# Fourth product of the linear cross-attention: two 128x128 products per batch against eight 32x32 products on the diagonal of the TensorE array

## The reference, cut to what matters

```python
Q, K, V = heads(ln(x) @ wq.T + bq), heads(c @ wk.T + bk), heads(c @ wv.T + bv)
score = einsum('bhqd,bhkd->bhqk', Q, K) / dk
ctx = einsum('bhqk,bhkd->bhqd', where(mask, -inf, score), V)
x = x + layernorm(ln(x) + ctx @ wo.T + bo)
```

## Time and profile before

| | |
|---|---|
| Median of 3 runs | 236.91 us (235.99 to 237.01) |
| Profiled execution, its own time | 236.04 us |
| Span in the profile | 234.2 us |
| TensorE busy | 220.6 us, 94% of the span |
| VectorE busy | 172.2 us, 74% |
| ScalarE busy | 125.0 us, 53% |
| GpSimd busy | 75.9 us, 32% |
| Granted TensorE clock | 0.998 of full speed (2.4 GHz) |

### The profile page before, as it was taken

One profiled execution on the slowest core, in us unless ns is written; L12 is line 12 of the kernel. 1 busy time (PEld: TensorE's weight loads), 2 busy tenths in 40 slices (PEclk: granted clock), 3 DMA queues, 4 the chain that ended last, 5 costly groups with the idle time before them and its releaser, 6 DMA issues.

```text
span 234.2 us, 5963 instructions
## 1 busy us (share of the span) xinstructions
PE 220.6 (94%) x2424; PEld 198.3 (85%) x2424; DVE 172.2 (74%) x370; ACT 125.0 (53%) x245; POOL 75.9 (32%) x101
## 2 busy tenths in 40 slices
PE   6998999999999998899999999999999999999991
PEld 6988798999999987778988999987778889988881
DVE  0669885886697699997975888978797674377353
ACT  3662961448346577757166798865643455740000
POOL 3012242030521617403526546693810022421011
PEclk9999999999999999999999999999999999999999
DMA  6799998986321613061302213032000000000001
GB/s 217 252 296 395 326 386 259 328 299 198 100 60 48 219 48 84 20 212 62 92 3 49 77 60 92 0 99 84 0 3 0 3 0 3 0 3 22 3 0 67
DMA packets 9435, 26.17 MB, mean 112 GB/s; under 512 B 1464, under 2 KB 2880, under 8 KB 9280
## 3 DMA queue, kind: packets, MB, share of 16 engines
q1 hardware_dynamic: 9120, 25.27, 32.9%
q10 hardware_dynamic: 288, 0.52, 0.6%
HBM read 25.27 MB, written 0.52 MB: 110 GB/s over the span
## 4 chain that ended last, share of the span: by engine, by line
PE 77%; DVE 6%; DMA 5%; ACT 5%; issue 4%; SPq 1%; POOLq 0%; POOL 0%; DVEq 0%; ACTq 0%
PE ps L707 72%; PE ps L710 5%; DMA w<-in_w 3%; DMA raw<-in_ctx 3%; ACT probT L518 1%; ACT ch L585 1%; DVE swapped L1258 1%; DVE straight L1262 1%; DVE straight L1259 1%; DVE mx L1232 1%; DVE prob L1242 1%; DVE swapped L1261 1%; ACT aT L518 1%; DVE sm L1240 0%; DVE Z L1304 0%
## 5 line engine op out<-in xcount | busy, mean ns | idle before, releaser
L707 PE MATMUL ps<-ch 128*128 128x130 f32 (+1 forms) x208 | 53.4, 272 | 1.6 <-DVE cl L1154 1.2
L707 PE MATMUL ps<-ch,cl 128*128 128x260 f32 (+1 forms) x208 | 52.1, 308 | 0.0
L707 PE MATMUL ps<-w,hT 128*128 128x512 f32 (+1 forms) x204 | 46.1, 382 | 0.0
L473 POOL TENSOR_TENSOR rstd<-ve,half_exp 128x1 f32<-128x1 f32 (+1 forms) x22 | 13.8, 626 | 88.6 <-DVE ve L1033 88.5
L707 PEld LDWEIGHTS ps<-w,hT 128*128 128x128 f32 x204 | 36.3, 188 | 7.2 <-issue 0.2
L707 PEld LDWEIGHTS ps<-ch 128*128 128x128 f32 (+1 forms) x208 | 39.6, 190 | 2.9 <-ACT ch L585 1.4
L1154 DVE TENSOR_TENSOR cl<-raw,ch 128x1024 fp32r<-128x1024 f32 (+4 forms) x31 | 31.8, 1056 | 10.9 <-ACT ch L585 10.6
L707 PEld LDWEIGHTS ps<-ch,cl 128*128 128x128 f32 (+1 forms) x208 | 39.2, 189 | 0.3
L585 ACT ACTIVATE ch<-raw 128x1024 fp32r<-128x1024 f32 (+4 forms) x31 | 27.4, 917 | 9.6 <-DMA raw<-in_ctx 8.4
L707 PE MATMUL ps<-xHL,dense 128*128 128x256 f32 x192 | 24.6, 285 | 0.0
L707 PEld LDWEIGHTS ps<-xHL,dense 128*128 128x128 f32 x192 | 23.5, 191 | 0.3
(11 more groups left out here) (157 smaller groups left out, 402.4 us busy)
## 6 DMA issues: line engine op xcount, KB each, us to landing
raw<-in_ctx SPq DMA_DIRECT2D x22, 512.0 KB, 4.4
raw<-in_w SPq DMA_DIRECT2D x8, 512.0 KB, 3.5
stage<-in_dense SPq DMA_DIRECT2D x4, 512.0 KB, 6.8
w<-in_w SPq DMA_DIRECT2D x4, 256.0 KB, 6.9
w<-in_w SPq DMA_DIRECT2D x1, 1024.0 KB, 8.6
mask<-in_mask SPq DMA_DIRECT2D x1, 800.5 KB, 7.6
raw<-in_ctx SPq DMA_DIRECT2D x8, 65.0 KB
raw<-in_ctx ACTq DMA_DIRECT2D x2, 256.0 KB, 4.8
```

The costliest lines, as they stand in the source:

```text
L473: pool.tensor_tensor(rstd[:, lo:hi], ve[:, lo:hi], half_exp[:, lo:hi], ALU.pow).then_inc(sem("rstd"), 1)
L707: return pe.matmul(o, l, r, start=start, stop=stop, skip_group_check=not check)
```

## The change

The matrix is kept as 32 columns per row, which is what `cross3` leaves: row `p` of `mb` holds the 32x32 block that its 32 rows share. A new constant `pair_heads` of 32 columns takes the place of `heads` at this spot (`heads` stays for another use, line 560). `cross4` then makes eight products per batch, one for each half and each group of 32 rows; product `r` reads rows `32r` to `32r+31` of `mb` and `q0T` and writes the same partitions of the bank. The list of steps, the semaphores and all other steps stay.

```diff
-for _name, _width in ((...), ("heads", P), ("causal", S), ...
+for _name, _width in ((...), ("heads", P), ("pair_heads", PAIR), ("causal", S), ...
...
+    put("pair_heads", ((p[:, None] // HD) % 2 == np.arange(PAIR)[None, :] // HD) * XSCALE)
...
-    mb, nxt = place("mb", [P, KC, P], at=nxt)
+    mb, nxt = place("mb", [P, KC, PAIR], at=nxt)
...
                     for ob in range(KC):
-                        last = mm(ps[:, CROSS_B[1], ob * S:(ob + 1) * S], mb[:, ob, :], q0T[:, ob, i * S:(i + 1) * S],
-                                  True, True)
+                        for r in range(P // PAIR):
+                            own_rows = slice(r * PAIR, (r + 1) * PAIR)
+                            last = mm(ps[own_rows, CROSS_B[1], ob * S:(ob + 1) * S], mb[own_rows, ob, :],
+                                      q0T[own_rows, ob, i * S:(i + 1) * S], True, True)
                     last.then_inc(sem("ctx"), 1)
...
                     pairs = ps[:, CROSS_B[0], D:D + KC * PAIR].rearrange("p (c n) -> p c n", c=KC)
-                    dve.tensor_tensor(mb[:, :, :].rearrange("p c (r n) -> p c r n", n=PAIR),
-                                      pairs.unsqueeze(2).to_broadcast([P, KC, P // PAIR, PAIR]),
-                                      const("heads").rearrange("p (r n) -> p r n", n=PAIR).unsqueeze(1).to_broadcast(
-                                          [P, KC, P // PAIR, PAIR]), ALU.mult).then_inc(sem("mb"), 1)
+                    dve.tensor_tensor(mb[:, :, :], pairs, pair_heads.unsqueeze(1).to_broadcast([P, KC, PAIR]),
+                                      ALU.mult).then_inc(sem("mb"), 1)
```

More of the change, by code:

```diff
@@ L44 @@
 _at = 0
-for _name, _width in (("ident", P), ("parity", 2), ("side32", 2), ("heads", P), ("causal", S), ("cos", S), ("sin", S),
+for _name, _width in (("ident", P), ("parity", 2), ("side32", 2), ("heads", P), ("pair_heads", PAIR), ("causal", S), ("cos", S), ("sin", S),
                       ("side", P), ("tile_of", T), ("iota", E)):
@@ L308, in layer @@
     ident = const("ident")
+    pair_heads = const("pair_heads")
     def column(name, k):
```

## The result

| | before | after |
|---|---|---|
| Median | 236.58 us (235.99 to 237.01, 8 runs) | 237.68 us (237.36 to 238.45, 8 runs) |
| Profiled execution, its own time | 236.04 us | 237.40 us |
| Span in the profile | 234.2 us | 235.6 us |

The ratio is 1.0055, with a 95% interval of 1.0041 to 1.0070: 1.1 us slower between the medians, where +0.4 us was forecast. The time lies in the forecast's range, but the loss is nearly three times the expected one. The forecast of 237.3 us stood on a median of 236.91 us for the kernel before; with the 236.58 us above it would have been 237.0 us.

A forecast was written before the change was run, and what follows sets the result against it. TensorE bounds most of the chain, VectorE's `mb` batches 4 and 7. Terms 0.8 - 0.07 - 0.4 + 0.05 = +0.38, rounded to +0.4 us on the median of 236.91, gave 237.3 us; range 235.7 to 239.0.

The forecast's parts named there:

- blocked pairs: Rival in `cross4`: two records of one product block each other, block 0.62 us, 238.9 us in all; chance 0.08.
- The block: The 16 records of a `cross4` step on PE: 0.39 us, as much as now.
- The way in and out: Around `cross4` on PE: 0.09 us going from whole products to parts, 0.03 us more behind for weights not loaded ahead.
- Six steps that pay in full: `cross4` of batches 0, 1, 2, 3, 5 and 6, bound by PE: 0.13 us more each, +0.8 us together.
- VectorE's 0.20 us: Each of the eight `mb` instructions 0.20 us shorter, on the chain only at batches 4 and 7: -0.4 us together.
- At batch 4: Chain on VectorE at `cross4`: the shorter `mb` gives its 0.20 us, PE has slack and costs nothing.
- Batch 7: `cross4` where PE waits for `mb`: way in hidden, -0.07 us on PE, and the 0.20 us of `mb` gained whole.
- Constants: `pair_heads` adds 16 KB ahead of the value weights, whose landing is in the chain: +0.05 us.
- The new places in memory cost nothing that a row shows: Tiles at new places in memory after the change: costed at nothing.
- The sum: All terms for the whole kernel: +0.38 us, rounded to +0.4; 0.0 to +0.9 with other block and `mb` values.
- Turns of the row groups: Rival in `cross4`: four row groups writing one bank are served one after another, +4.6 us, 241.5 us; chance 0.10.
- no-charge case: Rival in `cross4`: parts need only streaming, 0.25 us, ways in and out hidden; -1.3 us, 235.7 us; chance 0.12.

The follow-up runs named there:

- split_held: Kernel before with the eight 32x32 products, `mb` still 128 wide, half of GpSimd's piece 6 subtraction moved behind the inverse root of `xo` 3: ratio 1.0024.
- pad_only: Kernel before with 32 unused columns of constants where the change puts `pair_heads`, every tile behind them moved by 128 bytes: ratio 1.0030 (1.0019 to 1.0042).
- narrow_only: Kernel before with VectorE writing only 32 columns per half of `mb`, PE's products unchanged, output incomplete: ratio 1.0024 (1.0014 to 1.0035).

## Why the prediction was right, and where it was not

The time lies in the range, and the pieces of the changed step are near what was forecast, but the agreement is in part luck. The prediction had named as its own sign of being wrong a span that moves by over 1 us while the rows of the changed step stand, and that is what happened: 1.4 us, with a block of 0.36 us, a way in of 0.21 and `mb` at 0.22. The range took the measured time in because it had been drawn up to the rival of blocked pairs, 239.0 us, and not because a term allowed for what came.

- **The block**, taken at 0.39 us from `cross3` and `values`: 0.36 us. Bounding it by two steps with the same streamed columns per part was good; the 32x32 parts are 0.02 to 0.04 us better than these.
- **The way in and out**, 0.09 and 0.03 us: measured at 0.09 (0.21 less 0.12) and 0.03 (0.17 less 0.14). One PE-bound step costs 0.10 us in place of 0.13. This holds with the products alone, too: in split_held PE is 0.07 us late at the first `cross3` (27.71) and 0.49 us late behind the fourth `cross4` (64.97), again 0.10 for each of four steps. The prediction said that both rows of parts show the way in; only that of `values` does, as the earlier trace rows has no record in front of `cross3`.
- **Six steps that pay in full**, 0.8 us: batches 0 to 3 cost 0.41 us, but batches 5 and 6 together only 0.08 (from 0.16 at 89.34 to 0.24 at 126.10). Behind the `cross4` of batch 5 the chain leaves PE at 108.19 and goes over `ctxT` on ScalarE and VectorE. ScalarE's copy starts 0.16 us late (108.37 against 108.21). VectorE's addition behind it overlaps GpSimd's additions for `gpre` in both kernels; it took 0.67 us before (from 108.62) and 0.47 after (from 108.78). So it ends no later, and the next product on `ctxT` is only 0.08 us late:

```profile
110.19 1.13 PE L707 MATMUL ps<-w,ctxT 128*128 128x256 f32 x4 [0.26 <-ACT xT L518]
```

```profile
110.27 0.92 PE L709 MATMUL ps<-w,ctxT 128*128 128x256 f32 x3
```

- **VectorE's 0.20 us** per `mb`: 425 to 224 ns, exact. **At batch 4** it gave 0.10 to 0.13 us of the 0.20 forecast. What the chain pays is not the duration but the distance to the next instruction: the shuffle started 0.34 us behind `mb` before (83.48 to 83.82) and 0.21 us after (83.77 to 83.98). The 0.35 us stood in the earlier trace rows.
- **Batch 7**, -0.27 us of the sum, failed. The `cross4` there was early enough, and the products of `zT` did start 0.09 us before those of the kernel before (127.10 against 127.19). But I had priced `cross4` by PE and not asked who waits for its result and behind what. ScalarE copies `ctxT` only behind `xHL` and `xT` of the turn in front of it, and that turn was late by PE's 0.24 us. The chain after the change:

```profile
126.41 0.38 PE ps L712 x2
126.79 0.02 issue
126.82 0.39 ACT xHL L520
...
127.23 0.44 DVE xHL L1275
...
127.69 0.03 ACT xT L520
...
127.97 0.28 ACT ctxT L520
...
128.34 0.44 DVE ctxT L1205
```

  So PE waits at 128.82, and the 0.24 us go on whole to `Z`.
- **Constants**, +0.05 us: no run shows this term. The start of the first `cross3` spreads over 0.8 us from execution to execution, and the kernels with wider constants lie at both ends of it.
- **"The new places in memory cost nothing that a row shows"** is the step that failed most plainly: 0.5 us in the profile, 1.0030 (1.0019 to 1.0042) in pad_only. It was costed at zero because no row could show it, and not given a bound.
- **The sum assumed that a small delay stays small.** The sum that "goes from 0.0 to +0.9" moved each term by its own error, and gave none to one engine meeting another. (Its upper end is also not what its terms give: six steps at 0.14, batch 7 at -0.06, `mb` at -0.28 and the constants make +0.55 us.) The meeting at 131 us cost 0.7 us more, and narrow_only shows that it takes no delay of PE for it.
- **The rivals.** Turns of the row groups and blocked pairs are both out: four row groups write one bank in blocks of 0.36 us, where they asked for 0.99 and 0.62. So the sentence on row tiles and banks that the prediction cites for the turns does not hold for these four parts on the diagonal. The no-charge case is out by the 0.21 us of the way in.

In the sum of the profiled executions: -0.15 (opening) + 0.41 (batches 0 to 3) - 0.10 (batch 4) + 0.08 (batches 5 to 7) + 0.68 (meeting) - 0.03 (between 137 and 207 us) + 0.51 (pace) = 1.4 us, the difference of the spans. The mechanism that I forecast is 0.39 of it. That this is the +0.38 of the forecast is a coincidence: of its terms +0.8 came out as 0.49 and -0.47 as -0.10, and the two errors nearly cancel.

## What to carry to other kernels

Before a product is cut into parts of the array, count the columns that stream through each part; here a part streamed as many as before, the block took as long, and each step in parts cost about 0.1 us on the way in and out. Before a tile is widened, ask what lies behind it: a 128-byte shift changed the pace of products that the change never touched, and a shift of 256 did not. Price a term on a chain by the distance to the next start, not by the duration. In a kernel this tightly packed, look for instructions of VectorE with two memory operands that start within some tenths of a microsecond of a GpSimd instruction: another version can lose that race, and then a change is charged for it that had nothing to do with it.

## What the runs showed of the hardware that I had not expected

- The same instruction on VectorE took 0.47 us when it started 0.05 us ahead of GpSimd's subtraction, and 1.32, 1.42 and 1.53 us when it started 0.24, 0.14 and 0.03 us behind it. GpSimd then took 1.27 to 1.28 us in place of 1.58.
- 512-column fp32r products went from 3.79 to 3.89 us for 16 when the tile of their weights moved by 128 bytes, and back to 3.79 when it moved by 256.
- Four row groups with four different column groups write into one bank at the same time: 16 records of 64 columns in a block of 0.36 us.
